# First attention of a two-layer block: 1536 instead of 1024 of 1857 keys turned by DMA and VectorE, with a new order on every engine

## The reference, cut to what matters

```python
x = x + L0_xattn(layernorm(x), ctx_4096)     # the stage that changes
x = x + L0_ffn(layernorm(x)); x = x + L1_xattn(layernorm(x), ctx_4096); x = x + L1_ffn(layernorm(x))

def L0_xattn(latents, context):              # 4 batches of 256 tokens; 1601 context rows; width 512
    hidden = concatenate([context, latents]) # 1857 keys
    q, k, v = latents @ Wq, hidden @ Wk, hidden @ Wv   # 32 query heads and 4 key heads of 128
    attn = softmax(q k^T / sqrt(128))        # per query head: 256 x 1857
    return concat_heads(attn @ v) @ Wo
```

## Time and profile before

| | us |
|---|---|
| median of 3 runs (lowest, highest) | 3180.78 (3176.02, 3182.16) |
| the profiled execution: its time | 3190.52 |
| its span, first to last instruction | 3188.8 |
| first score matmul of the stage, last copy of an output | 544.2, 2117.0 |
| 1000 to 1200 us: busy PE, DVE, ACT, POOL | 200.00, 162.55, 138.08, 84.02 |

### The profile page before, as it was taken

One profiled execution on the slowest core, in us unless ns is written; L12 is line 12 of the kernel. 1 busy time (PEld: TensorE's weight loads), 2 busy tenths in 40 slices (PEclk: granted clock), 3 DMA queues, 4 the chain that ended last, 5 costly groups with the idle time before them and its releaser, 6 DMA issues. The chain is left out here.

```text
span 3188.8 us, 54146 instructions
## 1 busy us (share of the span) xinstructions
PE 3040.3 (95%) x18566; PEld 2702.9 (85%) x18566; DVE 2104.0 (66%) x3215; ACT 1733.4 (54%) x3277; POOL 908.0 (28%) x742
## 2 busy tenths in 40 slices
PE   8999998999999999999999999979989799998897
PEld 7888887899999999899998999968768788886786
DVE  4433343788888888788887888854454567766675
ACT  4433344676666666666666666642243344443472
POOL 0000121344444444444444444432200124440101
PEclk9999999999999999999999999999989799999998
DMA  7665696766777776677766777557540111111683
GB/s 253 216 214 200 207 289 200 152 159 161 165 160 158 163 157 164 150 165 158 160 160 155 160 158 163 127 148 238 190 160 32 57 29 41 41 41 30 236 289 129
DMA packets 375894, 497.03 MB, mean 156 GB/s; under 512 B 34316, under 2 KB 283452, under 8 KB 375640
## 3 DMA queue, kind: packets, MB, share of 16 engines
q1 hardware_dynamic: 373080, 485.40, 56.8%
q0 software_dynamic: 2560, 8.39, 0.8%
HBM read 225.57 MB, written 133.87 MB: 113 GB/s over the span
## 5 line engine op out<-in xcount | busy, mean ns | idle before, releaser
L725 POOL TENSOR_TENSOR a_t_lo<-a_turned,a_t_hi 128x512 fp32r<-128x512 f32 x512 | 649.7, 1291 | 937.9 <-ACT a_t_hi L854 937.9
L845 ACT ACTIVATE a_probs<-a_ps_s,a_neg_max 128x1024 f32<-128x1024 f32 (+1 forms) x512 | 529.2, 1034 | 474.7 <-DVE a_neg_max L897 468.8
L890 DVE TENSOR_REDUCE a_half_max<-a_ps_s 128x1 f32<-128x1024 f32 (+1 forms) x512 | 571.1, 1115 | 190.9 <-PE a_ps_s L742 186.7
L740 PE MATMUL a_ps_s<-a_k_buf,a_q_buf 128*128 128x512 f32 (+1 forms) x1024 | 420.1, 410 | 17.9 <-ACT a_probs L845 11.9
L741 PE MATMUL a_ps_s<-a_k_buf,a_q_buf 128*128 128x512 f32 (+1 forms) x1024 | 385.7, 377 | 0.0
L742 PE MATMUL a_ps_s<-a_k_buf,a_q_buf 128*128 128x512 f32 (+1 forms) x1024 | 384.8, 376 | 0.0
L926 DVE TENSOR_TENSOR a_x_lo<-a_ps_x,a_x_hi 128x512 fp32r<-128x512 f32 (+1 forms) x512 | 314.3, 614 | 106.6 <-ACT a_x_hi L863 106.6
L916 DVE STREAM_TRANSPOSE a_turned<-xn 128x512 f32<-128x512 f32 x512 | 357.4, 698 | 0.0
L472 DVE TENSOR_TENSOR p_out<-p_ps_j,p_out 128x512 fp32r<-128x512 f32 (+3 forms) x196 | 153.3, 782 | 302.4 <-ACT p_out L400 302.4
L400 ACT ACTIVATE p_out<-p_ps_j 128x512 fp32r<-128x512 f32 (+3 forms) x196 | 141.9, 724 | 311.4 <-PE p_ps_j L293 311.4
L740 PE MATMUL a_ps_o<-a_t_hi,a_v_buf 128*128 128x256 f32 x1024 | 298.8, 292 | 6.1 <-issue 3.6
(11 more groups left out here) (394 smaller groups left out, 7102.0 us busy)
## 6 DMA issues: line engine op xcount, KB each, us to landing
xn<-a_probs SPq DMA_DIRECT2D x1024, 128.0 KB, 3.4
a_q_all<-p_out SPq DMA_DIRECT2D x64, 512.0 KB
a_q_buf<-a_q_all SPq DMA_DIRECT2D x128, 256.0 KB, 3.2
a_k_buf<-a_k_all SPq DMA_DIRECT2D x64, 464.5 KB, 4.0
a_v_all<-p_out SPq DMA_DIRECT2D x56, 512.0 KB
a_k_all<-p_out SPq DMA_DIRECT2D x48, 384.0 KB
a_v_buf<-a_v_all SPq DMA_DIRECT2D x64, 256.0 KB
a_o_all<-a_o_part SPq DMA_DIRECT2D x128, 128.0 KB, 3.1
```

Of the source, the lines that this page charges most:

```text
L725: pool.tensor_tensor(t_lo[:, slot, :, :], turned[:, slot, :, :], t_hi[:, slot, :, :].bitcast(F32), ALU.subtract).then_inc(t_done, 1)
L740: pe.matmul(o, w_hi, m_hi, start=first, stop=False)
L845: act.activation(probs[j][u.a][:, lo:hi], s_flat[:, lo:hi], ACT.Exp, bias=neg_max[:, j:j + 1], scale=SCALE, accum_out=half_sum[:, bass.ds( ...
L890: dve.reduce_max(half_max[:, half:half + 1], s_flat[:, lo:hi], AX.X).then_inc(max_done, 1)
```

## The change

`RUN` goes from 256 to 384, so that 1536 keys are traded and turned (six pairs), and 321 stay plain (three blocks of 128, 128 and 65 keys in two pairs; six transposes on PE). The number of key blocks stays 15. The second copy of `traded` moves out of `xn` to a tile of its own; the plain ring shrinks to two slots. A trade now waits for both exponentials of its token half. The copy of the output moves from DVE to ACT. Every `step` has a new order.

```diff
-    RUN = 256
+    RUN = 384
...
-    RING, PRING, XBANKS = 4, 4, 2
+    RING, PRING, XBANKS = 4, 2, 2
...
+            traded = [by_run(xn[:, :, :].rearrange("p t d -> p (t d)")[:, 0:QT * TURNED]),
+                      by_run(sb("traded", [P, QT * TURNED])[:, :])]
...
-                    sp.wait_ge(probs_done, 4 * u.n + 2 * j + 1)
+                    sp.wait_ge(probs_done, 4 * u.n + 2 * j + 2)
...
+                def take_output(u):
+                    if not u.live:
+                        return
+                    act.wait_ge(tv_ps, TPAIRS * (u.n + 1))
+                    act.wait_ge(xv_ps, PPAIRS * (u.n + 1))
+                    wait(act, o_stored[u.a], 16 * u.use)
+                    act.activation(o_part[:, u.a, :], ps_o[:, u.a, 0:TOK], ACT.Copy).then_inc(copy_done, 1)
...
                 def step(b, r):
-                    v, w, l, z = Unit(b, r - 1), Unit(b, r - 2), Unit(b, r - 3), Unit(b, r - 4)
+                    v, l, z = Unit(b, r - 1), Unit(b, r - 3), Unit(b, r - 4)
+                    turn_plain(l, 0)
+                    turn_plain(l, 1)
                     weigh_turned(z, 2)
-                    weigh_plain(z, 2)
-                    turn_plain(l, 1)
-                    weigh_plain(z, 3)
+                    weigh_turned(z, 3)
+                    weigh_plain(z, 1)
+                    weigh_turned(z, 4)
                     scores(v, 0, 0)
-                    turn_plain(l, 2)
                     scores(v, 0, 1)
-                    weigh_turned(z, 3, last=True)
-                    turn_plain(l, 3)
+                    weigh_turned(z, 5, last=True)
                     weigh_turned(l, 0, first=True)
                     weigh_plain(l, 0)
                     weigh_turned(l, 1)
                     scores(v, 1, 0)
-                    turn_plain(w, 0)
                     scores(v, 1, 1)
-                    weigh_plain(l, 1)
...
                 def step(b, r):
-                    v, w, l, z = Unit(b, r - 1), Unit(b, r - 2), Unit(b, r - 3), Unit(b, r - 4)
-                    plain_low(l, 1)
+                    v, l = Unit(b, r - 1), Unit(b, r - 3)
+                    turn_traded(l, 0)
                     turn_traded(l, 1)
+                    plain_low(l, 0)
+                    turn_traded(l, 2)
                     maximum(v, 0, 0)
                     maximum(v, 0, 1)
                     negate_maximum(v, 0)
-                    turn_traded(l, 2)
-                    take_output(z)
-                    plain_low(l, 2)
+                    plain_low(l, 1)
                     turn_traded(l, 3)
+                    turn_traded(l, 4)
+                    turn_traded(l, 5)
                     maximum(v, 1, 0)
-                    plain_low(l, 3)
                     maximum(v, 1, 1)
                     negate_maximum(v, 1)
-                    plain_low(w, 0)
-                    turn_traded(w, 0)
```

More of the change, by code:

```diff
@@ L544, in grouped_attention_block @@
     VPIECES = sum(len(p) for p in VALUE_PIECES)
-    assert QT == 2 and len(CHUNKS) == 4 and HPG == 8 and TURNED <= 2 * BANK and TBLOCKS % 2 == 0 and WIDTH % 2 == 0
+    assert QT == 2 and len(CHUNKS) == 4 and HPG == 8 and TPAIRS == 6 and PPAIRS == 2 and TBLOCKS % 2 == 0 and WIDTH % 2 == 0
     assert PLAIN % 2 == 1 and TPAIRS * HEADS % RING == 0 and PPAIRS * HEADS % XBANKS == 0 and PPAIRS * HEADS % PRING == 0
@@ L606, in grouped_attention_block @@
             probs = [[sb(f"probs{j}{a}", [P, KEYS]) for a in range(2)] for j in range(QT)]
-            traded = xn[:, :, :].rearrange("p t d -> p (t d)")[:, 0:2 * QT * TURNED].rearrange("p (a j g r) -> p a j g r", a=2, j=QT, g=RUNS)
+            by_run = lambda rows: rows.rearrange("p (j g r) -> p j g r", j=QT, g=RUNS)
+            traded = [by_run(xn[:, :, :].rearrange("p t d -> p (t d)")[:, 0:QT * TURNED]),
+                      by_run(sb("traded", [P, QT * TURNED])[:, :])]
             turned = sb("turned", [P, RING, 2, TOK])
@@ L663, in trade @@
                     for c in range(RUNS):
-                        sp.dma_start(traded[SQ * c:SQ * (c + 1), u.a, j, :, :], probs[j][u.a][:, RUN * c:RUN * (c + 1)]
+                        sp.dma_start(traded[u.a][SQ * c:SQ * (c + 1), j, :, :], probs[j][u.a][:, RUN * c:RUN * (c + 1)]
                                      ).then_inc(trade_done[j][u.a], 16)
@@ L728, in step @@
                 def step(b, r):
[L729 to L735, removed]
+                    for p in range(TPAIRS):
+                        low(Unit(b, r), p)
+                run(pool, step, 0)
             @block.tensor
@@ L864, in plain_high @@
                                    ).then_inc(x_hi_done, 1)
+                def take_output(u):
[5 more added lines that the diff above has]
+                    act.activation(o_part[:, u.a, :], ps_o[:, u.a, 0:TOK], ACT.Copy).then_inc(copy_done, 1)
                 def step(b, r):
-                    u, v, w = Unit(b, r), Unit(b, r - 1), Unit(b, r - 2)
+                    u, v, w, z = Unit(b, r), Unit(b, r - 1), Unit(b, r - 2), Unit(b, r - 3)
                     exponentials(v, 1, 0)
+                    plain_high(w, 0)
+                    exponentials(v, 1, 1)
                     plain_high(w, 1)
-                    exponentials(v, 1, 1)
                     turned_high(w, 0)
                     turned_high(w, 1)
-                    plain_high(w, 2)
+                    turned_high(w, 2)
                     exponentials(u, 0, 0)
-                    plain_high(w, 3)
                     exponentials(u, 0, 1)
-                    turned_high(w, 2)
+                    take_output(z)
                     turned_high(w, 3)
-                    plain_high(v, 0)
+                    turned_high(w, 4)
+                    turned_high(w, 5)
                 run(act, step, 4)
@@ L916, in turn_traded @@
                     dve.transpose(turned[:, slot, :, :].rearrange("p k (q r) -> p k q r", r=SQ),
-                                  traded[:, u.a, :, :, 2 * SQ * p:2 * SQ * (p + 1)].rearrange("p j g (k r) -> p k (j g) r", k=2)
+                                  traded[u.a][:, :, :, 2 * SQ * p:2 * SQ * (p + 1)].rearrange("p j g (k r) -> p k (j g) r", k=2)
                                   ).then_inc(turn_done, 1)
```

## The result

The changed kernel takes 3219.38 us (median of 4 runs, 3209.21 to 3228.73) beside 3180.43 for the kernel before: 1.2% slower, ratio 1.0124, 95% interval 1.0089 to 1.0159. The forecast was 3096. The profiled execution took 3214.88, with a span of 3213.1.

The account below looks back on a forecast made before the run. PE and the chain from S2 to S3 were taken as balanced bounds; units 91 us less, drain +2 and DMA +4 gave net -85 from the profiled 3190.5, or 3096 us on the median of 3180.8; range 3062 to 3145.

Parts of the forecast that it names:

- The failed step: Trades between SBUF buffers: a DMA of 196,608 bytes would take 0.57 us by bytes, fitting under its issue of 0.62.
- The engines' part: Attention unit on PE, ACT, POOL and DVE: from 12.10 to 11.38 us, 91 us less over 127 units.
- the term that was taken: Length of an attention unit: 11.38 us, taken between 11.23 (PE without waits) and 11.48.
- the covers of ACT, POOL and DVE: Their work in a unit, laid out to fit under PE's 11.4 us: POOL's six L 7.6, DVE 10.1.
- Rival 3: Trades bound by bytes, slower: 1.25 us a DMA, 14.9 us a unit, some 3540 us; chance 0.06 well above.
- The term of +4 us for DMA: Heavier value loads in two steps of eight push the queue back: 0 to 1 us in each of 15 groups.
- What was to show it wrong: Signs in the changed profile: T waiting for DMA in every unit, SP trade issues far above 2.5 us, late maxima.
- the DMA share: Sign expected in the changed profile: share of the DMA engines about 0.85.

Follow-up runs that it names:

- e6_same64: The changed kernel with each DMA of a trade writing 64 neighbouring partitions, two rows in each (turned keys mixed up): 3165.32 us, ratio 0.9959 to the kernel before.
- e5_stride32: The changed kernel with each DMA of a trade writing every fourth partition, 32 in all, instead of 32 neighbours (turned keys mixed up): 3079.31 us, ratio 0.9682.
- e13_mixed_v: The changed kernel with value loads of turned keys each writing all 128 partitions, transposes unchanged, so weights meet other keys' values: 3193.67 us, ratio 1.0045.
- e1_short: The changed kernel with trades carrying 256 of the 384 columns of each run from the third unit on: 3081.51 us, ratio 0.9690 to the kernel before.

## Why the prediction was wrong

**The failed step** is the one on the trades: "With half as many bytes more, by bytes 0.57, by packets (as many as before) 0.38; both fit under the issue". The rate in it, 348 GB/s, was read from tenths of a us, and is that of the beginning of a trade only. A trade goes on at 140 to 180 GB/s, so a DMA of 196,608 bytes takes not 0.57 us but about 1.25 (at 157 GB/s), twice its issue of 0.62, and two trades about 10 of a unit's 12.45 us. The sentence "The 348 GB/s of the row contradict that for these trades" falls with it. The Trainium skill's rule (SBUF — State Buffer, Door 1: The DMA port swizzle) was right in kind, and the trace now agrees: 32 neighbouring partitions get about half of the wide rate, in these trades some 157 GB/s where the page measured 189. The Trainium skill, in the same section, has 64 neighbours only 4% above 32 (196 GB/s against 189), and e6_same64 agrees: its 0.43 us a unit are some 4% of the 10 us of two trades.

**The engines' part** held. With the trades spread or shortened the kernel takes 3079 to 3082 us, in the range of 3062 to 3145 and 14 to 17 below the forecast. In e5_stride32 N1 and N2 run from 550.9 to 2001.7:

```profile
L903 DVE TENSOR_SCALAR a_neg_max<-a_half_max x256: 212/214/216, 550.9 to 2001.7; 128x1 f32<-128x1 f32 x128
```

1450.8 us over 127.5 units is 11.38, the term that was taken; so six transposes, the covers of ACT, POOL and DVE, and the output copy on ACT at no cost were sized rightly in sum. In the unit shown above PE's parts fit too: S1 and S2 take 2.62 us (forecast 2.61), the 24 weighings behind them 2.84 (2.86), S3 starts 0.11 after those (0.25 at most), and the six transposes take 0.58 (0.65). The parts of the other engines were not tested one by one.

**Rival 3** had the mechanism, trades bound by bytes, and named the evidence for it, the landings of the earlier trace rows; it had a chance of 0.06 and a price of 3540, for 14.9 us a unit instead of 12.45. Its trades (16 x 5.0 us in eight units) are near what was measured. Mis-sized was the rest: 8 x 2.6 + 12.7 + 5.5 = 39 us in eight units, where 8 x 12.45 - 80 leaves 20. Outputs, queries and values stand in it at 151 GB/s, which the prediction read from 1110 to 1112 us as the rate of value loads. But a trade issued at 1107.21 still fills much of that stretch, and the one load issued behind it (first row below, line 585) writes all 128 partitions. The two loads that write 32 neighbours, issued at 1097.66, fall, by the bytes queued ahead of them, into the stretch of the second row. Both rows are of the kernel before:

```profile
1109.73 0.59 SPq L585 DMA_DIRECT2D a_v_buf<-a_v_all  x1
...
1100.25:1102.50 2.25, 2.25 (x14) 1.91 (x13) 1.55 (x3) 2.21 (x6) 0.05 (x1) 1.00 1.13 212
```

So narrow loads from DRAM ran at 212 GB/s (195 to 221 in four other groups), and the trades alone at about 160. The term of +4 us for DMA rests on the same misreading. An estimate for eight units from these rates: values 7.4 us at 212 and 0.9 at 348, keys 5.5, outputs and queries 9.0 at 348, 22.8 in all; the 99.6 measured then leave 4.8 for each trade. Wide value loads should bring 1.573 MB from 7.4 to 4.6 us, that is 2.8 in eight units and not 5.8; with e13_mixed_v eight units became shorter by (3219 - 3194)/16 = 1.6. The rest of that difference, and why trades are slower than loads to as many partitions, stay open.

**What was to show it wrong** came only in part: the prediction named "Waits of T for DMA in every unit". T waits for a trade in a part of the units (47 times from 700 to 2000 us, some 104 units); more often it is S1 that waits, for queries queued behind the trades (72 times). The plainer sign was the DMA share, 1.07 where "about 0.85" was named. S1's wait stood in the forecast only inside the DMA term ("the query load has about 1 to 2 us of slack"), at 4 us in all; the lower clock behind it stood in no part.

**The balance**: the engines gain 99 us (3180 to e1_short's 3082), the bytes take 138 back.

## What to carry to other kernels

Read a DMA's rate over the whole transfer, from issue to the last landing, not from the best slice of it; where two rows differed here (348 GB/s in a slice, 157 by landings), the slower one set the sum. See from the issues which transfer a slice belongs to: the 151 GB/s taken for value loads were largely a trade's. When a change sends more bytes to few partitions, add up the time of all queues for one period of the kernel and compare it with the period the engines would have, before crediting the engines with their gain. And when the DMA engines become full, look for the victim behind them: here mostly a load of 256 KB that the change had not touched.

## What the runs showed of the hardware

- Where a transfer lands matters more than how many partitions it reaches: every fourth partition gives 3079 us and 2.3 us to landing, 32 neighbours 3219 and about 6.
- 64 neighbouring partitions with two rows each lie between (3165), some 4% of the trades' time below 32. What makes the difference isn't settled.
- With the DMA engines full, trades to 32 neighbouring partitions went on at 140 to 180 GB/s, loads from DRAM to 32 neighbours at 195 to 221.
- Issuing DMAs that write neighbours alternately to both halves of the partitions saved 39 us with no other change.
- A second issuing queue made it slower (3239 against 3219).
- Loads whose slowest dimension is 4 long ran at 92 GB/s and a share of 0.27, and cost 320 us in this kernel.
- A transpose on DVE that reads 4-byte elements 48 bytes apart takes 1091 ns instead of 685.
